# First attention of a four-layer kernel: heads in the order 0, 2, 1, 3, first-pass units with the upper row half first

## What is computed

```python
    q = jnp.einsum('bnhd,ed->bnhe', data, Wq)
    k = jnp.einsum('bnhd,ed->bnhe', data, Wk)
    v = jnp.einsum('bnhd,ed->bnhe', data, Wv)
    scores = jnp.einsum('bqhd,bkhd->bhqk', q, k) / d ** 0.5
    attn = jax.nn.softmax(scores, axis=-1)
    Y = jnp.einsum('bhqk,bkhd->bqhd', attn, v).reshape(b, n, d)
```

## Time and profile before

| what | us |
|---|---|
| timed executions, median of 3 (lowest to highest) | 1042.45 (1040.85 to 1044.25) |
| profiled execution, span from first to last instruction | 1041.8 |
| PE busy | 903.3 (87%) |
| DVE busy | 804.5 (77%) |
| ACT busy | 612.7 (59%) |
| DVE row maxima of both attentions (L1025), 640 | 488.1 |
| ACT exponentials of both attentions (L982), 896 | 436.2 |

### The profile page before, as it was taken

One profiled execution on the slowest core, in us unless ns is written; L12 is line 12 of the kernel. 1 busy time (PEld: TensorE's weight loads), 2 busy tenths in 40 slices (PEclk: granted clock), 3 DMA queues, 4 the chain that ended last, 5 costly groups with the idle time before them and its releaser, 6 DMA issues. The chain is left out here.

```text
span 1041.8 us, 22164 instructions
## 1 busy us (share of the span) xinstructions
PE 903.3 (87%) x8501; PEld 460.0 (44%) x8501; DVE 804.5 (77%) x1600; ACT 612.7 (59%) x1280; POOL 199.4 (19%) x249
## 2 busy tenths in 40 slices
PE   5589999999999898975689999999989998777788
PEld 3212222222222223873345545555434776645568
DVE  7789999999899861647777878777851677799687
ACT  3228888888888686534146777676653446433552
POOL 2202033341202110540200001103000023123221
PEclk9659999999999899996679999999975998988899
DMA  2632435523426320111645544333100000000001
GB/s 77 189 82 65 113 101 117 117 56 90 110 83 130 116 39 15 53 50 41 191 104 144 151 103 103 86 82 89 42 6 23 12 1 2 1 0 1 4 6 36
DMA packets 62677, 73.71 MB, mean 71 GB/s; under 512 B 21143, under 2 KB 46864, under 8 KB 62558
## 3 DMA queue, kind: packets, MB, share of 16 engines
q1 hardware_dynamic: 48222, 49.23, 19.3%
q0 software_dynamic: 8576, 17.86, 7.0%
q10 hardware_dynamic: 5776, 5.22, 1.6%
HBM read 44.59 MB, written 18.16 MB: 60 GB/s over the span
## 5 line engine op out<-in xcount | busy, mean ns | idle before, releaser
L1025 DVE TENSOR_REDUCE a_negmax<-a_mbank 128x1 f32<-128x1024 f32 (+4 forms) x640 | 488.1, 817 | 73.8 <-PE a_mbank L829 36.0
L982 ACT ACTIVATE a_probs<-a_ebank 128x512 f32<-128x512 f32 (+3 forms) x896 | 436.2, 555 | 171.0 <-PE a_ebank L859 89.9
L850 PE MATMUL a_ebank<-b_moving,b_still 50*128 50x512 bf16 (+4 forms) x1280 | 270.7, 368 | 20.9 <-ACT a_probs L982 11.2
L821 PE MATMUL a_mbank<-a_moving,a_still 48*128 48x512 bf16 (+4 forms) x1280 | 262.8, 376 | 22.7 <-DVE a_negmax L989 10.0
L873 PE MATMUL a_acc<-a_probs,a_slot_v 128*32 128x512 f32 (+3 forms) x1792 | 226.9, 580 | 1.1 <-ACT a_probs L982 1.1
L850 PEld LDWEIGHTS a_ebank<-b_moving,b_still 58*64 58x64 bf16 (+1 forms) x1280 | 85.5, 102 | 257.0 <-ACT a_probs L982 200.6
L821 PEld LDWEIGHTS a_mbank<-a_moving,a_still 56*64 56x64 bf16 (+1 forms) x1280 | 69.0, 104 | 89.7 <-DVE a_negmax L1025 65.3
L859 PE MATMUL a_ebank<-a_bias_b,anti 64*64 64x176 bf16 (+4 forms) x1728 | 89.3, 233 | 0.0
L859 PEld LDWEIGHTS a_ebank<-a_bias_b,anti 64*64 64x64 bf16 x1728 | 70.6, 111 | 9.7 <-issue 1.5
L829 PE MATMUL a_mbank<-bias_a,anti 64*64 64x176 bf16 (+3 forms) x576 | 65.1, 237 | 0.0
L873 PEld LDWEIGHTS a_acc<-a_probs,a_slot_v 128*32 128x32 f32 x1792 | 35.8, 109 | 52.2 <-issue 41.0
(11 more groups left out here) (388 smaller groups left out, 1116.3 us busy)
## 6 DMA issues: line engine op xcount, KB each, us to landing
a_slot_v<-vo SPq DMA_DIRECT2D x16, 512.0 KB
b_moving<-stack SPq DMA_DIRECT2D x64, 96.0 KB
b_still<-stack SPq DMA_DIRECT2D x32, 192.0 KB
a_still<-stack SPq DMA_DIRECT2D x60, 96.0 KB, 2.8
a_moving<-stack SPq DMA_DIRECT2D x60, 96.0 KB, 2.7
expert<-in_expert_rows POOLq DMA_DIRECT2D x8, 578.0 KB, 4.1
a_bias_b<-trow SPq DMA_DIRECT2D x32, 66.0 KB
b_moving<-a_mparts SPq DMA_DIRECT2D x124, 2.0 KB
```

What stands on the lines that cost most here:

```text
L821: last = nc.tensor.matmul(mbank[COLS * c:COLS * (c + 1), bank, lo - left:hi - left], S.a_still[rows, q % 2, pr, at[c]:at[c] + COLS], S.a_m ...
L850: last = nc.tensor.matmul(ebank[COLS * c:COLS * (c + 1), s % NE, lo:512], S.b_still[rows, buf, pr, at:at + COLS], S.b_moving[rows, buf, h, ...
L982: nc.scalar.activation(probs[:, g % 2, j, lows[g]:512], ebank[:, s % NE, lows[g]:512], ACT.Exp).then_inc(p_full, 1)
L1025: nc.vector.tensor_reduce(to[:, at:at + 1], mbank[:, (index - 1) % NM, 0:right - left], AX.X, ALU.max, negate=True).then_inc(m_empty, 2 if ...
```

## The change

Three things, all for the first attention alone. The heads of a quad are taken in the order 0, 2, 1, 3 by TensorE's scores and ACT's exponentials, so the first two scores of a group read the lower row half and the last two the upper. The units alternate upper, lower. And the order in `turn` becomes: transposition or other non-unit entries first; score of head 0; first matmul of an upper unit; score of head 2; second matmul of that unit; score of head 1; values of the group before; score of head 3; the two matmuls of a lower unit. So that each group holds a whole pair of upper and lower unit, the start of every group moves on by one entry (`whole`), the opening too (26 entries, not 25).

```diff
-             for k in range(1 + h if causal else 1) for jj in range(2)]
+             for k in range(1 + h if causal else 1) for jj in (range(2) if causal else (1, 0))]
+    heads = range(QUAD) if causal else (0, 2, 1, 3)
...
-                        issue(scores(q, g, 0, buf))
-                        issue(scores(q, g, 1, buf))
-                        issue(first_pass(n, middle))
+                        n, end = whole(n), whole(end)
+                        while n < end and ordinary(n) is None:
+                            issue(first_pass(n, n + 1))
+                            n += 1
+                        upper, lower = (first_pass(m, min(m + 1, end)) for m in (n, n + 1))
+                        first = scores(q, g, 0, buf)
+                        next(first)
+                        next(upper, None)
+                        issue(first)
+                        second = scores(q, g, 1, buf)
+                        next(second)
+                        issue(upper)
+                        issue(second)
                         issue(scores(q, g, 2, buf))
                         previous(q, g)
-                        issue(scores(q, g, 3, buf))
-                        issue(first_pass(middle, end))
+                        issue(scores(q, g, 3, buf), lower)
+                        issue(first_pass(n + 2, end))
+
+            def ordinary(n):
+                use = uses[n % USES]
+                return None if n >= NQUAD * USES or type(use) is str else use[3]
+
+            def whole(n):
+
+                return n + 1 if ordinary(n) == 0 else n
...
-            issue(first_pass(20 if sort else 0, opening[0]))
+            issue(first_pass(20 if sort else 0, opening[0] if causal else whole(opening[0])))
...
-                    for j in range(QUAD):
-                        s = g * QUAD + j
+                    for i, j in enumerate(heads):
+                        s = g * QUAD + i
```

More of the change, by code:

```diff
@@ L806, in a_use @@
                 pr, qt, k, jj = uses[use]
-                if (qt, jj) == (0, 0):
+                if (qt, jj) == (0, units[0][3]):
                     if q:
@@ L825, in a_use @@
                     yield
+                    if not causal:
+                        continue
                     for c, (first, end) in enumerate(near):
@@ L832, in a_use, with scores @@
                 last.then_inc(m_full, 2 if (q, use) == (0, LATE - 1) else 1)
-            def scores(q, g, j, buf):
+            def scores(q, g, i, buf):
                 h, kt = groups[g]
-                s = g * QUAD + j
+                s = g * QUAD + i
+                j = heads[i]
                 pr, jj = j // 2, j % 2
@@ L976, in _ @@
                     act.wait_ge(p_empty, q * G + (g + 1))
-                    for j in range(QUAD):
-                        s = g * QUAD + j
+                    for i, j in enumerate(heads):
+                        s = g * QUAD + i
                         act.wait_ge(e_full, q * STEPS + (s + 1))
-                        if kt == 0 and j == 3 and q + h:
+                        if kt == 0 and i == 3 and q + h:
                             copy_out(2 * q + h - 1)
```

## The result

| us | before | after |
|---|---|---|
| timed executions, median of 4 (lowest to highest) | 1041.65 (1035.93 to 1044.25) | 1051.34 (1047.84 to 1052.54) |
| profiled execution, span | 1041.8 | 1046.0 |
| ratio of times, 95% interval | | 1.0127 (1.0085 to 1.0169) |

A second comparison, with more executions, gave 1.0100 (1.0055 to 1.0145). So the change costs 1.0 to 1.3%, some 10 to 13 us, where 3.0 was forecast, with an upper end of the range at 1051; the two medians of the table are 9.7 us apart, which is inside the interval. The direction was right; the forecast size was a quarter to a third of what came.

The account below looks back on a forecast made before the run. A 2.39 us loop of score, exponential, score and values, not DVE, bounds the first attention. Quads +1.6 and opening 1.3 give +2.9, rounded +3.0: span 1044.8, median 1045.5; range from near 1035 to 1051.

Parts of the forecast that it names:

- The loop of 2.39 us: First attention: score, exponential, score, values set each ordinary group at 0.42 + 0.65 + 0.32 + 1.00 = 2.39 us, not DVE.
- The ordinary group: Groups without special entries: no gain from pairing halves, 0.03 us lost in every second one, some 1 us in all.
- The transposition group: Groups 5 and 13: values to values 3.67 us instead of 2.39, net +0.7 to 0.8 each, 14 times.
- unit 3: Upper unit behind the transposition: waits for the reduction of the unit written just before, starting 1.91 us after score 3.
- Rival A: Transposition groups: the upper unit does not wait, so 11 us go away; faster, 1034; chance 0.13.
- The row waits: Quad openings and quad 6's group 8: late maxima rows; the change removes 9.6 us of waits, 5.7 and 3.9.
- rival B: Quad openings and quad 6: row copies take longer, so all 9.6 us of waits come back; 1055; chance 0.10.
- the 2.9: First attention: total forecast lengthening in us, +1.6 from the quads and 1.3 from the opening.
- The opening: Start of the first attention: one more unit ahead of the first score, bounds 0 and 1.5 us, 1.3 taken.
- rival C: Transposition groups: idle TensorE makes the clock fall, 2 to 3 us per event; 1048 to 1051; chance 0.15.
- rival E: TensorE: matmuls keep the skill's strict program order, so the 1 us ordinary-group loss is zero; 1044.5; chance 0.04.

Follow-up runs that it names:

- the halved reduction: Changed kernel, DVE taking 512 of 1024 columns for only the one unit ahead of each transposition; ratio 1.0013 to the kernel before.
- the second profile: Profile of the changed kernel run once more, with no further edit; ratio to the kernel before 1.0100.
- the experiment with the unmoved entries: Kernel before with heads 0, 2, 1, 3 and the change's interleaving, but units lower first and entries not moved on by one; ratio 1.0030.

## Why the prediction went as it did

**The loop of 2.39 us**: right. Halving the reductions left it unchanged, which also bears out that DVE's busy share was the wrong thing to read. (ACT, which is in the loop, is busy only 277 of the 365 us of the first attention, 76%, not over 80% as put ahead of the prediction.)

**The ordinary group**: right. 2.39 and 2.41 in turn, where 2.39 and 2.42 were worked out; 2.39 once DVE is quick.

**The transposition group**: right in mechanism and size: 3.67 forecast and measured, unit 3 at 1.92 for 1.91, and 0.83 net for each, where 0.7 to 0.8 were taken. Rival A, that unit 3 would not wait, is out; the halved reduction showed what it waits for.

**The row waits**: here is the step that failed, in the sentence "The 3.04 is mostly a wait for the maxima rows". In the quads 1 to 3 it is a wait for ACT, from the place in ebank that the last and the first score of two quads share. I compared the start of the score with the end of the split and took the distance for the transfer's length, without seeing the landing. Two things spoke against it: the bracket behind 195.22 in the earlier trace rows names ACT, and the line that I cited for a score's wait for an exponential, L843, holds the longer wait itself: `NE if s == 0 and (STEPS - 1) % NE == 0`. Also, a wait of the same size at one opening after another (3.03, 3.04, 3.04) points to a fixed order rather than to transfers. For the openings of the quads 5 and 7, group 8 of quad 6 and the last 0.4 us at quad 4 the step was right; these waits went, so rival B (1055, the row waits stay) is out as well. The opening of quad 6 was late for DVE's reciprocal too, which the prediction did not have.

The price: group 0 was put at 2.39 to 2.42 and is 2.92, 7 x 0.5 = 3.6 us. With 0.08 in group 8, which the sum left out and which is there in both kernels, and 0.07 in group 4 (the first unit of the next quad starts 0.70 us behind score 3, not 0.66; it goes to 2.39 when the reductions are halved), that is 7 x 0.65 = 4.6 of the 5.8 us by which the stage exceeds the 2.9. Quad 5's group 15, the reciprocal again, adds 0.8, the opening 0.2: together 5.6.

**The opening**: 1.3 taken, 1.51 measured, at the upper bound that I had given. The first values stand at 76.51, not at about 75.8, since the stage also began 0.55 us later in that profile.

**The sum against the median**: the rest of the difference is not in the stage's regular groups. The measured ratios stand for 10 and 13 us and their intervals reach down to 5.7 and 8.9; the 8.65 of the trace lie inside the one and just under the other. A fall of the clock as in the second profile (5.8 us, rival C's mechanism, though at the last transposition group alone and not at the others) would fill the gap if some executions have it; that is argued, not shown, and so the rest of the measured 10 to 13 us stays open. Rival C was priced at 2 to 3 us a fall; it was 5.8, since the half clock lasted four groups.

**The order of matmuls** (rival E): in the kernel before, the third score stands in the other half than the waiting unit and the group takes 2.81; in the experiment with the unmoved entries it stands in the same half and the group takes 3.03, one matmul of 512 columns more. The trace of the kernel before shows it directly, in the group of the earlier trace rows that takes 2.81:

```profile
190.09 0.39 PE L821 MATMUL a_mbank<-a_moving,a_still 48*128 48x512 bf16 x1
190.13 0.37 PE L850 MATMUL a_ebank<-b_moving,b_still 50*128 50x512 bf16 x1
190.31 0.38 PE L821 MATMUL a_mbank<-a_moving,a_still 48*128 48x512 bf16 x1
```

The score at 190.13, the last of the three ahead of values, starts between the two matmuls of a unit, and both of these stand ahead of the third score in program order. Had the order been strict, the third score would have stood behind the unit before as well, and the two groups would be alike in this. The rule of the Trainium skill that matmuls keep program order in start and end ("TensorE: Matmul & The Clock Gate", Part 3, "The mechanism") is not borne out by this pair. The trace of the changed kernel by itself doesn't tell, since there the third score is behind its unit in program order and in its half alike.

## What to carry to other kernels

Before a wait is charged to a transfer, look at which semaphores the waiting instruction has and which came last; a distance in time between two events that could be related is no evidence, and a wait of the same length again and again points to a fixed order. Where the number of places in a ring does not divide the work of a round, let the index run on over the rounds. When entries of two kinds share a ring of two places, moving them by one can put a consumer right behind the producer it waits for: work out the new distance for each special entry, as the ordinary ones say nothing about it.

## What the runs showed that I had not expected

An engine at 96% busy (DVE, 19.12 of 20 us) was not the bound, and with nearly half its work gone (10.62) the ordinary group was as long as before. A single idle stretch of TensorE of 1.32 us was followed by a fall to the half clock in one profile and not in another of the same kernel. And the second attention, which no edit touched, took between 262.3 and 270.7 us from the first to the last exponential in different profiles (263.2 and 269.8 for the same kernel). The first profile of the changed kernel had 263.3 where that of the kernel before had 269.8, which is why their spans differ by only 4.2 us: differences of spans of single profiles say little until such a stretch is taken out.
